# A fused attention and FP8 block: value and x blocks mixed, later second projections in the first full slot, two bank pairs in the last half slot, and two quarters of the last block normalized by ScalarE

## The reference

```python
x = x + proj(softmax(q k^T / 4) v)      # q, k, v from layernorm(x); 16 heads of 16
x = x + linear(fp8(layernorm(x)))       # rounded to float8_e4m3, fp8 weights, bias
```

## Time and profile before

| | |
|---|---|
| median of 3 runs (lowest, highest) | 969.11 us (968.7, 970.22) |
| the profiled execution, its own time | 968.59 us |
| its span, first to last instruction | 966.8 us |
| mean granted TensorE clock | 0.974 of full speed |
| PE matmul busy | 930.0 us (96%) |
| DVE, ACT, POOL busy | 843.8, 656.4, 515.9 us |

### The profile page before, as it was taken

How to read it: one execution, slowest core, us unless ns; L and a number is a source line. 1 busy time by engine, 2 the same in 40 slices (tenths; PEclk the granted TensorE clock), 3 DMA queues, 4 the chain that set the end, 5 groups by cost and what they waited for, 6 DMA issues and landing times.

```text
span 966.8 us, 16811 instructions
## 1 busy us (share of the span) xinstructions
PE 930.0 (96%) x5847; PEld 439.4 (45%) x5847; DVE 843.8 (87%) x1264; ACT 656.4 (68%) x1209; POOL 515.9 (53%) x528
## 2 busy tenths in 40 slices
PE   7799999999999999999999999999999999999993
PEld 4343444444444454544444444444444454433342
DVE  5678889898999989898998989899898989989846
ACT  3157777777777777767677776767777776776760
POOL 4522428467373847647383754738285573715222
PEclk9769999999999999999999999999999999999996
DMA  6971635438083554717265472817556280731010
GB/s 174 159 91 44 107 52 99 79 62 138 29 142 53 100 78 77 124 40 140 44 115 64 83 116 50 140 34 128 72 74 105 35 136 10 136 42 35 13 45 23
DMA packets 46350, 79.45 MB, mean 82 GB/s; under 512 B 10104, under 2 KB 13304, under 8 KB 46264
## 3 DMA queue, kind: packets, MB, share of 16 engines
q1 hardware_dynamic: 45976, 77.97, 47.1%
q10 hardware_dynamic: 288, 0.39, 0.3%
HBM read 18.42 MB, written 8.39 MB: 28 GB/s over the span
## 4 chain that ended last, share of the span: by engine, by line
PE 92%; DVE 2%; ACT 2%; SPq 1%; DMA 1%; issue 1%; ACTq 0%; POOL 0%; DVEq 0%; POOLq 0%
PE ps_t L551 29%; PE ps_o L591 26%; PE ps_m L426 10%; PE ps_s L570 8%; PE ps_m L475 5%; PE ps_m L499 5%; PE ps_m L531 3%; PE ps_m L412 1%; ACT pt L709 1%; PE ps_s L483 1%; DMA xin<-in_x 1%; SPq L309 1%; PE ps_m L514 1%; DVE mx L874 0%; PE ps_s L692 0%
## 5 line engine op out<-in xcount | busy, mean ns | idle before, releaser
L709 ACT ACTIVATE pt<-ps_t 128x512 f32<-128x512 f32 x1024 | 558.0, 598 | 213.9 <-PE ps_t L551 210.5
L874 DVE TENSOR_REDUCE mx<-ps_s 128x2 f32<-128x1024 f32 x512 | 615.3, 1209 | 57.4 <-PE ps_s L570 53.7
L551 PE MATMUL ps_t<-qs,ks 50*128 50x512 f32 x1024 | 391.9, 455 | 8.2 <-ACT pt L709 7.9
L570 PE MATMUL ps_s<-ks,qs 48*128 48x512 f32 x1024 | 380.7, 463 | 8.0 <-DVE nmax L923 4.1
L551 PEld LDWEIGHTS ps_t<-qs,ks 50*128 50x128 f32 x1024 | 164.0, 185 | 296.3 <-ACT pt L709 214.0
L591 PE MATMUL ps_o<-pt,vt 128*32 128x512 f32 x2048 | 272.6, 605 | 0.0
L1176 POOL TENSOR_TENSOR on<-ot,rden 128x256 f32<-128x256 f32 x63 | 39.3, 624 | 243.2 <-DVE rden L935 243.2
L570 PEld LDWEIGHTS ps_s<-ks,qs 48*128 48x128 f32 x1024 | 158.4, 188 | 18.9 <-issue 11.8
L426 PE MATMUL ps_m<-xnT_p,wqkv_p 128*128 128x512 f32 x360 | 109.9, 428 | 1.0 <-POOL xnT_p L1145 1.0
L1167 POOL TENSOR_TENSOR parts<-parts 128x512 f32<-128x512 f32 x60 | 81.3, 1356 | 4.9
L591 PEld LDWEIGHTS ps_o<-pt,vt 128*32 128x32 f32 x2048 | 40.4, 108 | 86.1 <-issue 85.1
(11 more groups left out here) (113 smaller groups left out, 763.3 us busy)
## 6 DMA issues: line engine op xcount, KB each, us to landing
qs<-parts SPq DMA_DIRECT2D x186, 128.0 KB, 4.6
ks<-parts SPq DMA_DIRECT2D x186, 128.0 KB, 5.4
xin<-in_x SPq DMA_DIRECT2D x16, 512.0 KB, 3.6
xres<-in_x SPq DMA_DIRECT2D x16, 512.0 KB, 5.8
out<-h SPq DMA_DIRECT2D x31, 256.0 KB, 2.1
qs<-nmax SPq DMA_DIRECT2D x256, 4.0 KB
pt<-in_qkv_wT SPq DMA_DIRECT2D x1, 768.0 KB, 5.2
qs<-parts SPq DMA_DIRECT2D x12, 64.0 KB, 3.6
```

Source lines behind the costliest of these rows:

```text
L551: nc.tensor.matmul(ps_t[:, g, :], ks[par][rows, slot, keys], qs[par][rows, slot, :], start=True, stop=True).then_inc(st_done, 1)
L570: done = nc.tensor.matmul(ps_s[:, s % 2, g, :], qs[par][rows, slot, queries], ks[par][rows, slot, :], start=True, stop=True)
L709: nc.scalar.activation(pt[n % 2][:, w % 2 + 2 * a, w // 2, :], ps_t[:, a, :], ACT.Exp, scale=SCALE).then_inc(exp_done, 1)
L874: dve.tensor_reduce(mx[:, r, :, s % QUARTER], ps_s[:, s % 2, :, :], AX_X, ALU.max).then_inc(max_done, 1)
```

## The change

- **Mixed blocks.** In place of 12 value matmuls at steps 20 and 22 and four transposes at 24 and 26, each of the steps 20, 22, 24 and 26 does `values_and_x`: six value matmuls into the first half of `ps_m` and two transposes of x into the second half. ACT makes two copies of 256 columns after each. So x is needed at step 20: the statistics move to steps 5, 7, 10, 12 and 13, and `layernorm_x` ahead of `low_oT` on POOL.
- **Start.** The transposes of block 1 move into slot 0 (banks `ps_o` and `ps_t`), behind five matmuls that nobody reads; the load of block 2 is issued first on SP, and its statistics are taken by DVE in slot 0. In slot 1 the third and fourth projections move to steps 14 and 16/18, 13 unread matmuls (`WARM_STEPS`) are added, the first `rows` is issued ahead of `stack`, and one stack of block 0's keys moves to ACT's queue.
- **Last half slot.** Odd steps of the second half of block 15 use `ps_s[:, 0]`, so `scores_t` waits for the exponential of two steps ago. `ln2_finish` moves to step 2, `round_last` to 4, `out_back` to 9, `copy_oT` to 12; POOL makes the layernorm first; the unread matmuls go from 13 to four.
- **Finish.** Both last `values` run ahead of `project_last`; 10 and 30 unread matmuls are added around the second half of it; ACT normalizes quarters 2 and 3 in two passes each.
- **Everywhere.** The negated mean is gone (subtract in place of add), and epsilon is added by a reduction over a third column of `mv1` and `mv2`.

The core of the diff (renumbered semaphore counts and declarations left out):

```diff
-LAST_ROUND = 8
+LAST_ROUND = 4
+LAST_END = 2
+LAST_BACK = 9
+LAST_COPY = 12
+FILL_VALUES = 10
+FILL_NORM = 30
...
-FILL_STEPS = range(3, 12)
+FILL_STEPS = (2, 4, 6, 8)
...
-PROJECT_QK_1 = ((4,), (6,), (8,), (10, 12))
+PROJECT_QK_1 = ((4,), (6,), (14,), (16, 18))
...
-PROJECT_V = (20, 22)
-TRANSPOSE_X = (24, 26)
-TRANSPOSE_X1 = (0, 2)
+VALUES_AND_X = (20, 22, 24, 26)
...
-LN1_SUM = (7, 12, 13, 15)
-LN1_END = 17
+LN1_SUM = (5, 7, 10, 12)
+LN1_END = 13
...
+WARM_SCORES = 5
+WARM_STEPS = (0, 1, 2, 3, 5, 7, 8, 9, 10, 11, 12, 13, 15)
+WARM_STEP = 1
...
+        def x_bank(b, c):
+            if b < 2:
+                return ps_t[:, c, :] if b == 0 else (ps_o[:], ps_t[:, 0, :])[c]
+            return ps_m[:]
+        def t_bank(b, s, g):
+            if b == B - 1 and s > HALF_STEPS and s % 2:
+                return ps_s[:, 0, g, :]
+            return ps_t[:, g, :]
...
             def first_slot():
+                load(2, 0)
...
-                for n in (2, 3):
-                    stack(0, 0, n)
-                load(2, 0)
+                stack(0, 0, 2)
...
+                if u == 1:
+                    rows(0, 0, 0)
...
-                if present(1):
+                if present(1) and u > 1:
...
         def _(pe):
-            bank_user = [None, 0, 0]
+            bank_user = ["bias", 0, 0]
             def take_bank(name, n, b):
...
+                elif last == "values_and_x":
+                    pe.wait_ge(v_ready, NJ * before + m + 1)
+                    if before < B - 1:
+                        pe.wait_ge(xnT_ready, 4 * (before + 1) + m + 1)
...
+                elif last == "bias":
+                    pe.wait_ge(const_v, 3)
...
-                for half in range(2):
-                    project_v(0, half)
-            def project_v(b, half):
...
+                for i in range(NJ):
+                    project_values(ps_t[:, i // 2, i % 2 * D:(i % 2 + 1) * D], 0, i)
+                pe.wait_ge(low_ready, 4)
+                pe.wait_ge(v_ready, 4)
+                for i in range(WARM_SCORES):
+                    nc.tensor.matmul(ps_s[:, 1, 1, :], wqkv_p[:, 0, 0, 0:P], wqkv_p[:, 0, 0, 0:S], start=True, stop=True)
+                for c in range(NC):
+                    transpose_x(1, c)
+            def project_values(bank, b, i):
+                tok = slice(i * P, (i + 1) * P)
+                for m, (pw, px) in enumerate(PAIRS):
+                    for c in range(NC):
+                        last = nc.tensor.matmul(bank, xnT_p[:, px, c, tok], wqkv_p[:, pw, c, 2 * D:3 * D],
+                                                start=(m == 0 and c == 0), stop=(m == 2 and c == NC - 1))
...
+            def values_and_x(u, i):
+                take_bank("values_and_x", i, u)
+                project_values(ps_m[:, 0:D], u, i)
+                if u < B - 1:
+                    c, half = i // 2, i % 2
+                    pe.wait_ge(xn_ready, u + 2)
+                    for j in range(2):
+                        last = nc.tensor.transpose(ps_m[:, D + j * P:D + (j + 1) * P],
+                                                   xn[:, 2 * half + j, c * P:(c + 1) * P], ident[:])
+                    last.then_inc(xt_done, 1)
...
-                if past(2 * STEPS * b + 2 * s + g - 1):
+                if b == B - 1 and s == HALF_STEPS + 1:
+                    pe.wait_ge(max_done, STEPS * b + STEPS - 1)
+                elif b == B - 1 and s > HALF_STEPS:
+                    pe.wait_ge(exp_done, 2 * STEPS * b + 2 * s + g - 3)
+                elif past(2 * STEPS * b + 2 * s + g - 1):
...
+                nc.tensor.matmul(t_bank(b, s, g), ks[par][rows, slot, keys], qs[par][rows, slot, :],
...
+                    if u == 1 and s in WARM_STEPS:
+                        unread(WARM_STEP)
...
-                    if s in PROJECT_V and present(0):
-                        project_v(u, PROJECT_V.index(s))
-                    if s in TRANSPOSE_X and u > 0 and present(-1):
-                        transpose_x(u + 1, TRANSPOSE_X.index(s))
+                    if s in VALUES_AND_X and present(0):
+                        values_and_x(u, VALUES_AND_X.index(s))
...
-                        for i in range(2 - s % 2):
-                            nc.tensor.matmul(ps_s[:, 0, i, :], wqkv_p[:, 0, 0, 0:P], wqkv_p[:, 0, 0, 0:S],
-                                             start=True, stop=True)
+                        pe.wait_ge(nmax_split, 8 * (u - 2) + 8)
+                        nc.tensor.matmul(ps_s[:, 1, 0, :], wqkv_p[:, 0, 0, 0:P], wqkv_p[:, 0, 0, 0:S],
+                                         start=True, stop=True)
...
+                    last = nc.tensor.matmul(ps_m[:, 0:D], b_v_rep[:, t, :], wproj[:, t, :],
...
+            def unread(count):
+                for i in range(count):
+                    nc.tensor.matmul(ps_t[:, 1, :], wqkv_p[:, 0, 0, 0:P], wqkv_p[:, 0, 0, 0:S], start=True, stop=True)
...
             def finish(b):
...
+                values(b, b % 2, UNITS - 1, 1)
...
-                pe.wait_ge(nmax_split, 8 * b + 8)
...
-                values(b, b % 2, UNITS - 1, 1)
...
+                unread(FILL_VALUES)
...
+                unread(FILL_NORM)
...
-            def copy_v(b, par, half):
-                act.wait_ge(v_done, 2 * b + half + 1)
+                nc.scalar.activation(pt[n % 2][:, w % 2 + 2 * a, w // 2, :], t_bank(b, s, a), ACT.Exp, scale=SCALE).then_inc(exp_done, 1)
+            def copy_v(b, par, i):
+                act.wait_ge(v_done, NJ * b + i + 1)
+                if b < B - 1:
+                    act.wait_ge(xt_done, 4 * (b + 1) + i + 1)
...
-                nc.scalar.copy(vt[par][:, 2 * half:2 * half + 2, :, 0:HD],
-                               bank.rearrange("p (j h e) -> p j h e", j=2, h=H)).then_inc(v_ready, 1)
+                nc.scalar.copy(vt[par][:, i, :, 0:HD],
+                               ps_m[:, 0:D].rearrange("p (h e) -> p h e", h=H)).then_inc(v_ready, 1)
+            def copy_x_half(b, i):
+                c, half = i // 2, i % 2
+                act.wait_ge(xt_done, 4 * b + i + 1)
+                nc.scalar.copy(xn[:, 2 * half:2 * half + 2, c * P:(c + 1) * P],
+                               ps_m[:, D:2 * D].rearrange("p (j m) -> p j m", j=2)).then_inc(xnT_ready, 1)
...
-                copy_v(0, 0, 0)
-                copy_v(0, 0, 1)
+                copy_first_v(0)
+                copy_first_v(1)
+                for c in range(NC):
+                    copy_xnT(1, c)
+                act.wait_ge(low_ready, 4)
+                for r, part in enumerate(K_PARTS):
+                    for g in range(2):
+                        rows = slice(HALF * g + HD * r, HALF * g + HD * (r + 1))
+                        act.dma_start(ks[0][rows, NS:2 * NS, :].bitcast(F32),
+                                      parts[HALF * g:HALF * (g + 1), 3, part, :]).then_inc(stacked[1][0], 16)
...
-                    if s == COPY_OT[0] and present(2):
+                    if s == (LAST_COPY if u == LAST_SLOT else COPY_OT[0]) and present(2):
...
-                        if s == PROJECT_QK[n][-1] and present(0):
+                        if s == (PROJECT_QK if u > 1 else PROJECT_QK_1)[n][-1] and present(0):
...
-                    if s in PROJECT_V and present(0):
-                        copy_v(u, par, PROJECT_V.index(s))
-                    if s in TRANSPOSE_X and u > 0 and present(-1):
-                        copy_xnT(u + 1, TRANSPOSE_X.index(s))
+                    if s in VALUES_AND_X and present(0):
+                        copy_v(u, par, VALUES_AND_X.index(s))
+                        if u < B - 1:
+                            copy_x_half(u + 1, VALUES_AND_X.index(s))
             def finish(b):
...
+                act.wait_ge(ln2_ready, b + 2)
+                act.mul(nm2[:], mv2[:, 2:NJ, 0], -1.0).then_inc(nm2_ready, 1)
+                act.wait_ge(nm2_ready, 1)
+                for j in range(2, NJ):
+                    nc.scalar.activation(hn[:, j, :], h[:, j, :], ACT.Identity, bias=nm2[:, j - 2:j - 1]).then_inc(centred, 1)
+                act.wait_ge(rs2_ready, b + 2)
+                for j in range(2, NJ):
+                    act.wait_ge(centred, j - 1)
+                    act.wait_ge(hn_ready, b + j - 1)
+                    nc.scalar.activation(hn[:, j, :], hn[:, j, :], ACT.Copy, scale=rs2[:, j:j + 1]).then_inc(hn_ready, 1)
...
         def _(dve):
+            def finish_bias():
+                dve.wait_ge(bias_done, 1)
+                dve.tensor_tensor(b_proj[:], ps_m[:, 0:D], b_proj[:], ALU.add).then_inc(const_v, 1)
...
-            def finish_bias():
-                dve.wait_ge(bias_done, 1)
-                dve.tensor_tensor(b_proj[:], ps_o[:, 0:D], b_proj[:], ALU.add).then_inc(const_v, 1)
+                finish_bias()
+                for j in range(NJ):
+                    ln1_sum(2, 0, j)
+                ln1_finish(2)
...
-                dve.tensor_scalar(nm1[:], mv1[:, :, 0], -1.0, None, ALU.mult).then_inc(ln1_ready, 1)
```

(57 more changed lines are left out.)

96 lines of the change are left out of this document (41 added, 55 removed).

## The result

The changed kernel takes 998.58 us (992.49 to 1000.92, 4 runs) against 969.08 before: ratio 1.0293, interval 1.0245 to 1.034. It is 3% slower, where 946 was forecast. The profiled execution has a span of 990.5 us, 23.7 above the one before. I read it at the same three places as before, and first the page: busy times, then the chain that ended last by engine, here and in the kernel before.

A forecast was written before the change was run, and what follows sets the result against it. PE was taken to bound the steady stretch, the scores_t-exponential round trip the last half slot, nothing the start. Gains of 8 + 5 + 10 = 23 off 968.6 give 945.6, with the runs' median 946; range 938 to 951, chance 0.56.

The forecast's parts named there:

- Dropping the negated mean: Both layernorms: one small DVE instruction less each, counted as nothing.
- The sign of being wrong: Steady slots: a slot no shorter than 55.76 us, or PE waiting on POOL's x, would show the forecast wrong.
- x late at step 20: Steady slots: x, expected 1.8 us early, comes late and PE stands in 14 slots; kernel slower; chance 0.04.
- Steady stretch, 5 gained: Slots 2 to 15: mixed pairs gain 7.6 us, narrow copies cost 2.8; bounds 13 gained and 6.4 lost.
- The 2.8 for the narrow copies: Steady stretch: two narrow ACT copies delay the exponentials, 56 pairs x 0.05 us, counted on PE.
- rival two: Steady stretch: narrow copies stand on PE's path; at 0.25 us a pair 957; chance 0.12 of over 951.
- Start, 8 gained: Slots 0 and 1: 10.3 us gained if the clock stays up, 3.5 lost if it stays at 0.50; 8 taken.
- 6.5 at full clock: Slot 1, steps 0 to 15: 21.6 us with the charge, against 28.16, a gain of 6.5.
- the first rival: Slot 1: the clock falls, the start loses 3.5 us and the kernel takes 957; chance 0.20.
- The rule cited from the Trainium skill: Start: sustained matmul activity releases the throttle, so unread matmuls would bring the whole 10.3 us, kernel near 944.
- End, 10 gained: Last half slot and finish: 7.9 us gained before DVE's start, net 1.9 in the finish; bounds 3 and 12.
- my 7.9: Last half slot: with two bank pairs PE and ACT run side by side; DVE starts at 935.8, not 943.90.

The follow-up runs named there:

- add_both: Changed kernel with both POOL layernorms (xn and hn) put back to adding a negated mean, which DVE negates; 949.23 us, ratio 0.9796 to before.
- add_pool: Changed kernel with both layernorms back to the add, and x's mean negated by POOL behind the power instead of by DVE; 945.55 us, ratio 0.9757.

## Why the prediction was wrong

**The step that failed** is "Dropping the negated mean takes one small DVE instruction off each layernorm; I count nothing." The diff showed the other half of that edit, the add turned into a subtract in POOL's two loops, and I priced the new line by the old row: "from 501.39 it needs 3.53 us", with the 2.18 of the earlier trace rows. Measured, the form costs 1.22 us for 0.55, 2.7 us for each group of four and 5.3 a slot in POOL's list. It made the difference of 49.4 us between the changed kernel and add_both, and it is enough to make the kernel before 29.9 slower. The sign of being wrong that stands on record came in both its forms: a slot of 58.55, and PE waiting on POOL's x. The nothing was wrong the other way too: the DVE instruction dropped was worth 3.7 us in this order (949.23 to 945.55), 4.9 in the middle by the profiles.

**The rival that came nearest** was x late at step 20, at 0.04. Its wait is there (12.7 us in twelve slots) and in slot 9 its arithmetic holds: 5.3 more in the list, less the 1.8 spare and the 1.6 by which PE itself was late (1.39 and 0.23), leaves 1.9; 1.66 was measured. In six of the twelve slots the wait is 1.28 to 1.80 us; in the other six, where the clock had fallen behind `hq` and made PE later still, it is 0.46 to 0.53. But I looked for lateness in the new order alone, and never at `hq`, which comes ahead of x in the same list and costs PE more (18.1 us). With the add, the margin was about as forecast. In add_pool's slot 9 `xn` ended at 493.60 and its transposes began at 495.09, 1.5 us to spare for my 1.8 (1.6 in most slots; 2.26 in add_both, where POOL has no negation to do):

```profile
491.43 2.17 POOL L1222 TENSOR_SCALAR xn<-xin,nmx,rs 128x256 f32<-128x256 f32 x4 [0.33 <-POOL nmx L1210]
```

```profile
495.09 0.38 PE L521 MATMUL ps_m<-ident,xn 128*128 128x128 f32 x2
```

**Steady stretch, 5 gained.** Forecast 0.45 a slot from mixing; 0.50 measured. The 2.8 for the narrow copies was a cost that isn't there: the pairs take 3.46, and rival two falls. By an estimate from the figures of the Trainium skill (ScalarE: Activation LUTs, What ACT_TABLE_LOAD costs) each split copy costs 93 ns; two copies of 0.37 for one of 0.59 are 0.05 to 0.15 on ScalarE, which agrees, but the pairs show that none of it reaches PE. The middle of add_pool is 8.4 shorter than before, against 7.6 without that charge.

**Start, 8 gained.** 7.8 in add_pool (64.62 to 56.83): 3.8 up to step 16 (its first `scores_t` at 46.98 for 50.78), where I had summed 6.5 at full clock, and 4.0 in steps 16 to 21, where I had 3.8. (The windows of the earlier trace rows end step 19 some 0.9 us late, at the second `scores_t` of step 20; that shifts time between two of my terms, not their sum.) The clock did fall, to 0.59 over the window from 34.30 to 46.50, with PE busy 11.31 of 12.20 us, as the row at 50.50 had warned:

```profile
34.30:46.50 12.20, 11.31 (x27) 5.19 (x27) 8.85 (x9) 0.64 (x1) 4.29 (x7) 0.59 0.99 159
```

It came back at step 16, so the loss of the first rival, which let it stay down, did not come. The rule cited from the Trainium skill (TensorE: Matmul & The Clock Gate, Part 1) would have had it stay up, and the trace does not agree. Without the unread matmuls the start is still 6.7 earlier. By the trace, what carries it is the work moved, though no run tests the moves one by one: DVE's wait of 4.74 us has no counterpart in slot 1, and the steps from 16 on run at clock 1.00 instead of 0.50. Why the clock falls where it does stays open.

**End, 10 gained.** 9.65 in all (51.49 to 41.84). The half slot takes 21.06 where DVE's start stood 28.59 after step 1 before: 7.5 for my 7.9 (943.90 less the 935.8 given there is 8.1). The second bank pair alone is 4.6 of it; the rest is what was moved around it. The finish gives 2.1 for my 1.9, of which ScalarE's normalization is 0.9.

So with the adds kept, and the negation where POOL can't hold it up, the forecast would have stood: 945.55 for 946. That it is so near is in part luck: by the profiles the three stretches gave 25.8 us for the 23 summed, and add_pool's runs lie between 942.9 and 947.95.
